# Attention scores from two float32r halves on 64-row tiles instead of three bf16 thirds, with three score banks, grouped values and unrolled attention

## What is computed

```
x = L0_attn_x
xn = layernorm(x)
Q = (xn @ Wq.T).reshape(16, 4, 1024, 16)      # K and V likewise
scores = einsum('hbqd,hbkd->hbqk', Q, K)
out = einsum('hbqk,hbkd->hbqd', softmax(scores), V).reshape(4, 1024, -1)
y = out + xn
attn = (y - mean(y, (1, 2))) / sqrt(var(y, (1, 2)) + 1e-5)
ffn = sum over 8 experts e of gates[:, e] * ((xn @ w_in[e].T) @ w_out[e].T)   # gates: softmax of the two largest of 8 logits
result = x + attn + ffn
```

## Time and profile before

| | us |
|---|---|
| three runs, median (lowest to highest) | 1115.41 (1113.98 to 1117.44) |
| the profiled execution, its span | 1116.5 |
| TensorE busy | 1077.7 |
| VectorE busy | 850.5 |
| ScalarE busy | 654.6 |
| GpSimd busy | 172.1 |
| the chain of work that ended last: TensorE, SyncE's queue, DMAs | 50%, 18%, 14% of the span |

### The profile page before, as it was taken

One profiled execution on the slowest core, in us unless ns is written; L12 is line 12 of the kernel. 1 busy time (PEld: TensorE's weight loads), 2 busy tenths in 40 slices (PEclk: granted clock), 3 DMA queues, 4 the chain that ended last, 5 costly groups with the idle time before them and its releaser, 6 DMA issues.

```text
span 1116.5 us, 25452 instructions
## 1 busy us (share of the span) xinstructions
PE 1077.7 (97%) x7752; PEld 550.3 (49%) x7752; DVE 850.5 (76%) x1171; ACT 654.6 (59%) x1256; POOL 172.1 (15%) x364
## 2 busy tenths in 40 slices
PE   7999999999999999999999999999999999999995
PEld 6888878887663333333333333333333333333332
DVE  6333377777897888888878888888888888888876
ACT  3333311211216777777777777777777777777775
POOL 2221033533320011001001101001100101100100
PEclk9999999999998999999999999999999999999998
DMA  8999699888520111111111111111111111111104
GB/s 268 386 325 334 223 169 201 164 201 172 150 67 25 47 37 37 47 37 37 46 37 35 45 40 35 42 43 34 40 45 35 40 46 34 37 47 35 38 20 151
DMA packets 127227, 107.48 MB, mean 96 GB/s; under 512 B 58848, under 2 KB 96480, under 8 KB 127200
## 3 DMA queue, kind: packets, MB, share of 16 engines
q1 hardware_dynamic: 73696, 64.93, 20.5%
q10 hardware_dynamic: 53504, 42.21, 13.9%
HBM read 68.56 MB, written 38.54 MB: 96 GB/s over the span
## 4 chain that ended last, share of the span: by engine, by line
PE 50%; SPq 18%; DMA 14%; issue 4%; DVE 1%; ACT 1%; POOL 0%; POOLq 0%; ACTq 0%; DVEq 0%
PE ps L981 15%; PE ps L1013 13%; SPq L328 11%; PE ps L1003 11%; PE ps L1025 10%; DMA max_d<-mt 8%; DMA qf<-max_d 5%; SPq L341 4%; SPq L332 3%; PE ps L1034 2%; DMA xttl<-xtl_d 1%; ACT wp L600 0%; DVE stage L900 0%; SPq L360 0%; DVE negm L775 0%
## 5 line engine op out<-in xcount | busy, mean ns | idle before, releaser
L775 DVE TENSOR_REDUCE negm<-ps 128x1 f32<-128x1024 f32 x512 | 603.5, 1219 | 124.6 <-PE ps L1003 123.7
L600 ACT ACTIVATE wp<-ps 128x512 f32<-128x512 f32 x1024 | 555.9, 595 | 223.1 <-PE ps L1013 222.8
L1013 PE MATMUL ps<-qf,kf 99*128 99x512 bf16 x1024 | 324.3, 386 | 16.6 <-DMA qf<-max_d 14.3
L1025 PE MATMUL ps<-wp,vb 128*17 128x256 f32 x4096 | 272.7, 383 | 0.0
L1003 PE MATMUL ps<-kf,qf 96*128 96x512 bf16 x1024 | 265.9, 380 | 1.5 <-DVE negm L775 1.5
L1013 PEld LDWEIGHTS ps<-qf,kf 99*128 99x128 bf16 x1024 | 81.6, 97 | 243.5 <-issue 108.6
L1003 PEld LDWEIGHTS ps<-kf,qf 96*128 96x128 bf16 x1024 | 98.2, 97 | 125.2 <-issue 5.8
L1025 PEld LDWEIGHTS ps<-wp,vb 128*17 128x17 f32 x4096 | 94.0, 97 | 109.6 <-issue 60.8
L981 PE MATMUL ps<-mth,xtth 128*128 128x512 f32 x256 | 104.8, 409 | 3.0 <-DMA xttl<-xtl_d 1.9
L981 PE MATMUL ps<-mtl,xtth 128*128 128x512 f32 x256 | 102.0, 399 | 0.0
L981 PE MATMUL ps<-mth,xttl 128*128 128x512 f32 x256 | 101.9, 398 | 0.0
(11 more groups left out here) (107 smaller groups left out, 644.9 us busy)
## 6 DMA issues: line engine op xcount, KB each, us to landing
wp<-w_in SPq DMA_DIRECT2D x16, 512.0 KB, 4.7
wp<-w_out_t SPq DMA_DIRECT2D x16, 512.0 KB, 6.0
qk_d<-stage ACTq DMA_DIRECT2D x8, 1024.0 KB, 4.7
third_d<-wp ACTq DMA_DIRECT2D x32, 256.0 KB, 2.6
qf<-third_d SPq DMA_DIRECT2D x64, 96.0 KB
kf<-third_d SPq DMA_DIRECT2D x64, 96.0 KB
v_d<-vstage ACTq DMA_DIRECT2D x8, 544.0 KB, 3.7
vb<-v_d SPq DMA_DIRECT2D x128, 34.0 KB, 2.7
```

The costliest lines, as they stand in the source:

```text
L600: nc.scalar.activation(wp[:, kt % 4, h * HALF:(h + 1) * HALF], ps[:, ST_BANK[h], :], ACT.Exp).then_inc(exp_done[h], 1)
L775: nc.vector.tensor_reduce(negm[:, par, qt:qt + 1], ps[:, b:b + 2, :].rearrange("p b c -> p (b c)"), AX.X, ALU.max, negate=True).then_inc(m ...
L1013: nc.tensor.matmul(ps[:, ST_BANK[h], :], kf[0:SR, u, kt * P:(kt + 1) * P], qf[0:SR, u, h * HALF:(h + 1) * HALF], start=True, stop=True).th ...
L1025: last = nc.tensor.matmul(ps[32 * j:32 * j + VW, PV_BANK, 0:POS // 4], vb[:, par, kt, :], wp[:, kt % 4, j * (POS // 4):(j + 1) * (POS // 4 ...
```

## The change

- **Splitting.** A float32 value is split into two float32r halves, high and low. Scores are hi x hi + hi x lo + lo x hi: 3 x 16 = 48 rows (FR), and two rows for the maxima, split in two halves likewise (SR = 50). ScalarE makes the high halves, GpSimd one subtraction for each; four tiles of 512 KB a chunk are stored into `feat_d`.
- **64-row tiles.** `qf` holds the query features twice, on partitions 0 to 49 and 64 to 113. `kf` (now in the space of `xth`) holds keys 0 to 511 on the first and keys 512 to 1023 on the second. A maxima pair multiplies the same queries by both halves of the keys, a score pair a key tile of each half by the same 512 queries, one matmul on each half of the array's rows.
- **Banks.** Scores use three banks (4, 5, 7) by turns; a pair waits until all exponentials but one have been done. The transposes have no bank of their own; they take turns in the maxima's banks, after the fifth maxima pair of every second head.
- **Order.** The unit is (j, h), key tiles j and j + 4 by query half h. TensorE: scores, maxima of one query tile, scores, maxima, then the value products of the two key tiles of the group before. Attention is written out for all 64 heads, with constant addresses.
- **DMAs of a head.** Eight feature loads for six (the same 576 KB in all), two loads of maxima rows for three.

```diff
-    TERMS_Q = (0, 1, 2, 0, 1, 0)
-    TERMS_K = (0, 0, 0, 1, 1, 2)
-    FR = DH * len(TERMS_Q)
-    SR = FR + 3
+    TERMS = 3
+    FR = DH * TERMS
+    SR = FR + 2
+    ROWS = P // 2
...
-        qf = sb("qf", [SR, SLOTS, POS], BF16)
-        kf = sb("kf", [SR, SLOTS, POS], BF16)
+        qf = sb("qf", [P, SLOTS, POS], FP32R)
+        kf = xth[:].rearrange("p a k t -> p (a k) t")
...
-        ST_BANK = (4, 5)
+        ST_BANK = (4, 5, 7)
...
-            for first_row, terms in ((0, 3), (3, 2), (5, 1)):
-                rows = slice(first_row * DH, (first_row + terms) * DH)
-                yield qf, rows, third_d[0, 0:terms, block_rows, :]
-                yield kf, rows, third_d[1, first_row // 2 if terms < 3 else 0, block_rows, :
-                                        ].unsqueeze(0).to_broadcast([terms, DH, POS])
+            for half in range(2):
+                first = half * ROWS
+                keys = slice(half * HALF, (half + 1) * HALF)
+                yield (qf, slice(first, first + 2 * DH), slice(0, POS),
+                       feat_d[0, 0, block_rows, :].unsqueeze(0).to_broadcast([2, DH, POS]))
+                yield qf, slice(first + 2 * DH, first + FR), slice(0, POS), feat_d[0, 1, block_rows, :]
+                yield kf, slice(first, first + 2 * DH), slice(0, HALF), feat_d[1, 0:2, block_rows, keys]
+                yield kf, slice(first + 2 * DH, first + FR), slice(0, HALF), feat_d[1, 0, block_rows, keys]
...
-                for c in range(3):
-                    sp.dma_start(qf[FR + c:FR + c + 1, slot, :].rearrange("o (t q r) -> o t q r", q=4, r=32),
-                                 max_d[par].rearrange("(q c t) r -> c t q r", q=4, c=4)[c:c + 1]
+                for half in range(2):
+                    first = half * ROWS + FR
+                    sp.dma_start(qf[first:first + 2, slot, :].bitcast(FP32).rearrange("c (t q r) -> c t q r", q=4, r=32),
+                                 max_d[par].rearrange("(q c t) r -> c t q r", q=4, c=4)[0:2]
                                  ).then_inc(mrow_in[slot], 16)
...
+            for n in range(NB - 1):
+                if n:
+                    sp.wait_ge(pv_done, NKT * n)
+                values(n + 1)
+                max_rows(n + 1)
+                if n + SLOTS < NB:
+                    for half in range(2):
+                        sp.wait_ge(st_ready[half], NKT * (n + 1))
+                    features(n + SLOTS)
...
+            def exps(n, j, h):
+                unit = NKT * n + 2 * j + h
+                for b in range(2):
+                    act.wait_ge(st_ready[b], unit + 1)
+                    used = NKT * n + 2 * j + b - 4
+                    if h == 0 and used >= 0:
+                        act.wait_ge(pv_done, used + 1)
+                    nc.scalar.activation(wp[:, j % 2 * 2 + b, h * HALF:(h + 1) * HALF], ps[:, ST_BANK[(2 * unit + b) % 3], :],
+                                         ACT.Exp).then_inc(exp_done, 1)
...
+            def max_scores(n, qt):
+                u, turn = n % SLOTS, max_turn[n, qt]
                 if qt == 0:
-                    pe.wait_ge(feat_in[u], 96 * (i + 1))
+                    pe.wait_ge(feat_in[u], 128 * (n // SLOTS + 1))
+                free_turn(turn)
+                for half in range(2):
+                    rows = half_rows(half, FR)
+                    last = nc.tensor.matmul(ps[:, MAX_BANK[turn % 2] + half, :], qf[rows, u, qt * P:(qt + 1) * P],
+                                            kf[rows, u, :], start=True, stop=True)
+                last.then_inc(turn_ready, 1)
+
+            def scores(n, j, h):
+                u, unit = n % SLOTS, NKT * n + 2 * j + h
+                if j == 0 and h == 0:
+                    pe.wait_ge(mrow_in[u], 32 * (n // SLOTS + 1))
+                if unit:
+                    pe.wait_ge(exp_done, 2 * unit - 1)
+                for half in range(2):
+                    rows = half_rows(half, SR)
+                    nc.tensor.matmul(ps[:, ST_BANK[(2 * unit + half) % 3], :], kf[rows, u, j * P:(j + 1) * P],
+                                     qf[rows, u, h * HALF:(h + 1) * HALF], start=True, stop=True
+                                     ).then_inc(st_ready[half], 1)
...
+            for n in range(NB):
+                for j in range(NKT // 2):
+                    for h in range(2):
+                        scores(n, j, h)
+                        if n + 2 < NB:
+                            max_scores(n + 2, 2 * j + h)
+                        if j == 2 and h == 0 and n % 2 == 0 and n:
+                            to_token_rows(n // 2 - 1)
...
+                    for b in range(2):
+                        if j:
+                            sum_values(n, j - 1, b)
+                        elif n:
+                            sum_values(n - 1, NKT // 2 - 1, b)
```

More of the change, by code:

```diff
@@ L323, in _, with features @@
                     next_xt(XS * k + slot, slot)
-            def features(n, slot):
-                for dst, rows, source in feature_loads(n):
-                    sp.dma_start(dst[rows, slot, :], source).then_inc(feat_in[slot], 16)
-            def values(n, par):
+            def features(n):
+                slot = n % SLOTS
+                for dst, rows, columns, source in feature_loads(n):
+                    sp.dma_start(dst[rows, slot, columns].bitcast(FP32), source).then_inc(feat_in[slot], 16)
@@ L372, in _ @@
-            with sp.Fori(0, NB // SLOTS - 1) as i:
-                for u in range(SLOTS):
-                    step(i, u)
-                    step_features(i, u)
-            for u in range(SLOTS - 1):
-                step(NB // SLOTS - 1, u)
+            values(0)
+            max_rows(0)
+            for s in feat_out:
+                sp.wait_ge(s, 32 * NC // 2)
+            for n in range(NB - 1):
[7 more added lines that the diff above has]
+                    features(n + SLOTS)
@@ L412, in _ @@
                                             ALU.add).then_inc(xn_saved[p], 1)
+            for p in range(2):
+                pool.wait_ge(v_ready[p], 2 * NC)
+                pool.wait_ge(xt_stored[p], 32 * NC // 2)
+            nc.gpsimd.memset(kf.bitcast(FP32), 1.0).then_inc(att_const, 1)
             with pool.Fori(0, NC // 2) as k:
@@ L617, in _ @@
-            for u in range(SLOTS):
-                step(0, u, before=u > 0)
-            with act.Fori(1, NB // SLOTS) as i:
-                for u in range(SLOTS):
-                    step(i, u)
-            pv_out_at(NB // SLOTS - 1, SLOTS - 1)
+            for s in feat_out:
+                act.wait_ge(s, 32 * NC // 2)
+            def exps(n, j, h):
[7 more added lines that the diff above has]
+                                         ACT.Exp).then_inc(exp_done, 1)
@@ new lines, in pv_out @@
+            def pv_out(n):
+                act.wait_ge(pv_done, NKT * (n + 1))
+                if n >= 2:
+                    act.wait_ge(turn_ready, row_turn[n // 2 - 1] + 1)
+                nc.scalar.copy(ot[:, :, n % 2, :], ps[:, PV_BANK, 0:4 * TB].rearrange("p (g t) -> p g t", t=TB)
+                               ).then_inc(pv_evac, 1)
+            for n in range(NB):
+                for j in range(NKT // 2):
+                    exps(n, j, 0)
+                    exps(n, j, 1)
+                    if j == 0 and n:
+                        pv_out(n - 1)
@@ L796, in statistics @@
             def statistics(pair):
                 dve.wait_ge(y_done, pair + 1)
[L798 to L815 removed]
+                nc.vector.bn_stats(ystat[:, pair, :], xn[:, pair, :]).then_inc(ystat_done, 1)
@@ L823, in _ @@
                         nc.vector.memset(ps[:, PV_BANK, 0:POS // 4], 0.0).then_inc(att_const, 1)
-                    maxima(n, None, n, qt)
+                    maxima(n, qt)
                     if n == 1 and qt == 1:
-                        max_transpose(0, 0, 0)
-            for u in range(SLOTS):
-                step(0, u, pair=0 if u >= 2 else None)
-            with dve.Fori(1, NB // SLOTS - 1) as i:
-                for u in range(SLOTS):
-                    step(i, u, pair=2 * i + u // 2 - 1)
-            last = NB // SLOTS - 1
-            for u in range(2):
-                step(last, u, pair=2 * last - 1)
+                        max_transpose(0)
+            for n in range(NB - 2):
+                for qt in range(NKT):
+                    maxima(n + 2, qt)
+                    if qt == 1:
+                        max_transpose(n + 1)
+                    if n % 2 == 0 and n and qt == 4:
+                        normalise(n // 2 - 1)
+                    if n % 2 == 1 and n > 1 and qt == 1:
+                        statistics((n - 1) // 2 - 1)
             def aggregate(part, entries):
@@ new lines, in sum_values @@
+            def sum_values(n, j, b):
+                if j == 0 and b == 0:
+                    pe.wait_ge(vb_in[n % 2], 32 * (n // 2 + 1))
+                    if n:
+                        pe.wait_ge(pv_evac, n)
```

(7 more changed lines are left out.)

302 lines of the change are left out of this document (103 added, 199 removed).

## The result

The changed kernel takes 1266.46 us (median of 4 runs, 1256.09 to 1276.23) where the kernel before takes 1114.70 (1113.18 to 1117.44): 1.134 times as long, 95% interval 1.128 to 1.140. The ratios and intervals leave out executions that lie more than 1.5% above the fastest of the same kernel, here the one of 1276.23 us. The forecast was 1074, range 1025 to 1127.

A forecast was written before the change was run, and what follows sets the result against it. TensorE's order and SyncE's loop were taken to bind together, 24.08 us for two heads. Falling to 22.7 over 31 pairs saves 43 us, less 1.6 before attention: 1075 on the profiled span, about 1074 us, range 1025 to 1127.

The forecast's parts named there:

- What bounds the kernel before: Attention, two heads: TensorE's order sets 23.5 us, SyncE's loop adds the last 0.6; VectorE is third with 20.4.
- Phases before attention, +1.6 us: Before attention: less splitting gains nothing, sixteen maxima pairs among the expert matmuls cost 1.6 us in all, 5 either way.
- A pair in 0.23 us, 0.10 for a load not hidden: TensorE: a pair's halves run side by side in 0.23 us; after a wait or tiling change its weight load adds 0.10.
- Rivals 1 to 3: Load hidden: 1030 us, chance 0.20; pair's loads one after another: 1120, 0.17; halves not side by side: 1184, 0.10.
- The group, 2.82 us: TensorE in attention: a group of two key tiles takes 2.82 us instead of 2.87, standing 0.6 for ScalarE's exponential.
- Transposes add nothing: TensorE: transposes, some 0.50 us, fit inside the wait for the exponential, so their 0.49 us for two heads goes.
- SyncE's loop, 11.6 us: SyncE's part takes 11.6 us; with TensorE's 10.15 it makes 21.75 for two heads, 0.8 under TensorE's 22.56.
- The upper bound: SyncE's loop: dearer feature loads (+2.4 us) and loads of maxima (+1.5) make at most 25.65 us for two heads.
- Rival 4: SyncE's queue binds in attention at its upper bound, 25.65 us for two heads: 1165 us, chance 0.07.
- Rival 5: TensorE's clock falls for its new idle time in the groups: 1116 + 430 us at worst; chance 0.04, shared with anything unforeseen.
- What would show it: Signs in the trace: right, groups of about 2.8 us; wrong, pairs 0.4 us apart, TensorE waiting for queries, half clock.

The follow-up runs named there:

- e4: The kernel before, with its six feature loads of three, two and one term issued as twelve of one term: 1110.45 us, 0.997 of before.
- e1: The changed kernel with twelve one-term feature loads a head instead of eight, same bytes: 1105.82 us, 0.992 of the kernel before.
- e2: The changed kernel without the feature loads of heads 4 to 63, which reuse the first four heads' features: 1114.74 us, 1.000 of the kernel before.
- e3: The changed kernel with the maxima pair ahead of each group's wait for the exponential issued three times: 1240.83 us, 1.115 of the kernel before.
- e10: The changed kernel with only the queries' two-term load split into two one-term loads, the keys' kept: 1104.69 us, 0.994 of the kernel before.
- e11: The changed kernel with one-term loads, both maxima pairs mostly before the second score pair, six feature loads before the maxima's store, six after their load: 1048.56 us.
- e9: The changed kernel with SyncE's order alone changed to store of maxima, values, load of maxima, features last: 1460.91 us, 1.315 of the kernel before.
- e7: The changed kernel with a maxima pair issued nine times ahead of every second head's first scores: 1218.30 us, 1.097 of the kernel before.

## Why the prediction was wrong, step by step

- **What bounds the kernel before**: not contradicted, and hardly tried. In e4 the store lands 1.3 us earlier, behind 1.2 us more of issue, and the time stays.
- **Phases before attention, +1.6 us**: failed, 17.5. The sixteen pairs among the expert matmuls cost what was said: with one-term loads the first scores start 1.1 us later than before. What was missing is that the initial feature loads stand in SyncE's queue among the token tiles, so that slow loads there stop TensorE (e1, e2).
- **A pair in 0.23 us, 0.10 for a load not hidden**: held. A maxima pair follows a score pair after 708.01 - 707.67 = 0.34 us, as forecast (0.33). A pair behind its like follows after 0.23: in e3 six matmuls take 0.86 us where two take 0.40. Rivals 1 to 3 fall with it.
- **The group, 2.82 us**: held, 2.84.
- **Transposes add nothing**: failed, 0.62 us for two heads (707.67 - 704.21 = 3.46, less 2.84). They do fit into the wait for the exponential, as said: the second score pair starts at 705.46. But they take a turn in the maxima's banks, and the maxima pair behind them then needs the reduction of the pair just before them: it comes at 706.26, not at 705.46 + 0.33 = 705.79. With 2.83 and 3.47, TensorE needs 23.3 us for two heads, not 22.56, and e10, with most of the trouble gone, shows what that leaves: two heads 23.4, attention 752.0 us, 18 less than before (43 were forecast), 3 us more ahead of it and 3 behind the last scores.
- **SyncE's loop, 11.6 us**: here the prediction broke. The issue of eight loads was right (4.54 for 4.4), the values too (1.2 for 1.3), and so was the load of maxima (2.24 for 2.0). "Store of the maxima until it can be read, 2.90" was carried over from before and was 5.2 to 5.8: in these runs the landing of a store is no constant of the store, but hangs on what is in front of it on the slowest of its engines. "I take mine, as the loads match old ones in rows and terms" named the right comparison and missed what differs: a term in float32 has twice the bytes, so that 384 KB a head travel in two-term loads, where it was 192 KB in three-term and 128 KB in two-term ones. All features of a head are 576 KB now and were 384 KB (twice 96, 64 and 32), and not "the same 576 KB in all" as stated under the change. The kernel before had a sign of it as well: of its store issued at 666.00, 14 parts had landed by 667.66 and the last two at 668.78 and 668.88, behind the last of its features and values (668.36 and 668.71), so that 2.90 was itself a time behind other loads. The upper bound was made for issue and for the load of maxima, not for the landing of the store.
- **Rival 4** (SyncE's queue binds, 25.65) was near to what happened, with a chance of 0.07, for another cause, and its 1165 lacked the second step.
- **Rival 5** (the clock falls) was dismissed by the wait inside the group, and rightly as far as that wait brings no fall by itself (e1), though it lengthens those that happen (e3). But the clock was weighed on its own. It comes as the second step of rival 4: SyncE's loop makes TensorE stand in one piece, as it had partly ahead of 335.4 in the earlier trace rows, and the fall follows. The two together are the 1266; a rival that makes TensorE wait in one piece has to be priced with the half clock behind it.
- **What would show it**: the list had both signs under "wrong", TensorE waiting for the query tile and half clock in attention.

**How the loss divides** can be estimated from the traces. Against e1 (749 us) attention is 155 us longer. The waits of TensorE's matmuls for the load of maxima are 64 us in the changed kernel and 3 in e1. Half clock in attention is 259 us for 14, and a group takes 4.47 us there for 2.83, so that these 245 us cost about 90. The sum, 151, leaves little else; the clock took more than the waits that brought it down. The 134 us against the kernel before are less by the 20 us that the new order gains in e1.

**Open:** an exact division, since waits and clock change each other; and what the kernel before would gain from e11's order on SyncE, which wasn't tried.

## What to carry to other kernels

Before a load is priced by its bytes and its issue, look at the outermost count of its access pattern: one that counts 2 ran on two DMA engines here, at 41 to 57 GB/s, and what was issued within the next microseconds, a small store above all, landed behind it. Price a landing by what is in front of it, and draw each loop that a reordering creates, not only the one that it shortens. Where TensorE will wait in one piece at every turn of a loop, as here for 0.9 to 2.9 us, price the half clock behind it too.

## What the runs showed of the hardware that was not expected

- A transfer of [2 x 16 rows] keeps the DMA share at 0.11 to 0.14 (two of sixteen engines) and 41 to 57 GB/s; with loads of 16 rows the last load of a head lands 1.9 us after its issue (e11) for 6.9 (e9).
- A store of 16 KB lands in 16 parts: 14 of them by 1.7 us (median) and the last two at 5.1 and 5.3 when two-term loads stand ahead of it, all by 1.7 when one-term loads do (e1).
- SyncE's issue itself stops when such loads back up: 6.05 and 6.64 us for two loads at L314 (up to 4.09 for one), where a load in one term is issued in 0.42.
- Two float32r matmuls of 50 rows on the two halves of the array stream side by side: the next pair follows 0.33 us behind one with an uncovered weight load.
- 198 waits of up to 0.5 us left the clock at full speed (e1). With 0.9 to 2.9 us of idle matmuls at every second head as well, it fell behind each of these 30 waits and was at half for 285 of 1268 us; 2 us of filler matmuls in them brought 48 us back (e7). With the short waits filled and the long ones left it fell at 29 of the 30, for 150 us in all (e3).
